# An adaLN block of two Mamba-2 layers and a channel mix: modulated rows made inside the first layer's loop

## What is computed

```python
mod = (silu(c) @ wmod).reshape(8, 6, 1, 512)
sa, ca, ga, sb, cb, gb = (mod[:, n] for n in range(6))
ga = (2 * (ga >= 0) - 1) * maximum(abs(ga), 0.25)      # gb likewise
h = layernorm(x) * (1 + ca) + sa
x = x + ga * mamba_layers(h)           # 2 layers, each: h + mamba2(layernorm(h) * w + b)
h = layernorm(x) * (1 + cb) + sb
x = x + gb * channel_mix(h)            # receptance, key, value products, token shift
```

## Time and profile before

| | us |
|---|---|
| time, median of 3 runs | 4278.69 |
| lowest and highest of them | 4275.23, 4281.79 |
| the profiled execution's own time | 4276.1 |
| its span, first to last instruction | 4274.3 |
| PE busy | 4005.1 (94%) |
| DVE busy | 3465.9 (81%) |
| ACT busy | 2899.9 (68%) |
| POOL busy | 2026.9 (47%) |

### The profile page before, as it was taken

How to read it: one execution, slowest core, us unless ns; L and a number is a source line. 1 busy time by engine, 2 the same in 40 slices (tenths; PEclk the granted TensorE clock), 3 DMA queues, 4 the chain that set the end, 5 groups by cost and what they waited for, 6 DMA issues and landing times. The chain is left out here.

```text
span 4274.3 us, 100194 instructions
## 1 busy us (share of the span) xinstructions
PE 4005.1 (94%) x38872; PEld 3600.5 (84%) x38872; DVE 3465.9 (81%) x5227; ACT 2899.9 (68%) x4898; POOL 2026.9 (47%) x1572
## 2 busy tenths in 40 slices
PE   4599999999999999969999999999999996799999
PEld 1599999899999999958999999999999995577777
DVE  8688888888888888868888888888888885666664
ACT  4577777677777777747777777777777773666664
POOL 7344444444444444424444444444444444566664
PEclk6799999999999999979999999999999998899999
DMA  8400000000000000020000000000100002222220
GB/s 327 142 31 31 31 31 31 31 31 31 31 31 31 31 33 32 26 96 29 31 31 31 31 31 31 31 33 35 37 31 31 31 26 85 82 97 97 85 83 33
DMA packets 115764, 220.03 MB, mean 51 GB/s; under 512 B 10792, under 2 KB 20520, under 8 KB 114472
## 3 DMA queue, kind: packets, MB, share of 16 engines
q1 hardware_dynamic: 115376, 214.25, 14.1%
HBM read 146.97 MB, written 67.24 MB: 50 GB/s over the span
## 5 line engine op out<-in xcount | busy, mean ns | idle before, releaser
L508 PE MATMUL l_ring<-l_u_hi,l_wi_lo 128*128 128x256 f32 x4608 | 1318.2, 286 | 22.2 <-ACT l_raw L754 12.4
L508 PE MATMUL l_ring<-l_u_lo,l_wi_hi 128*128 128x256 f32 x4608 | 1296.6, 281 | 0.0
L508 PE MATMUL l_ring<-l_u_hi,l_wi_hi 128*128 128x256 f32 x4608 | 1296.0, 281 | 0.0
L1008 DVE SCALAR_TENSOR_TENSOR l_xc<-l_raw,l_prm,l_xc 128x256 f32<-128x256 f32 x1536 | 958.3, 668 | 96.4 <-ACT l_xc L763 78.2
L508 PEld LDWEIGHTS l_ring<-l_u_hi,l_wi_lo 128*128 128x128 f32 x4608 | 873.1, 189 | 48.3 <-issue 16.9
L508 PEld LDWEIGHTS l_ring<-l_u_lo,l_wi_hi 128*128 128x128 f32 x4608 | 874.0, 190 | 11.7
L1199 POOL TENSOR_TENSOR l_g<-l_g 128x512 f32<-128x512 f32 (+2 forms) x384 | 355.6, 926 | 1096.1 <-ACT l_g L824 1076.0
L508 PEld LDWEIGHTS l_ring<-l_u_hi,l_wi_hi 128*128 128x128 f32 x4608 | 873.9, 190 | 0.0
L1170 POOL TENSOR_TENSOR l_rhs<-l_cum,l_small 32x1024 fp32r<-32x1024 f32 x256 | 497.5, 1952 | 154.1 <-PE l_wide L570 103.8
L1190 POOL TENSOR_TENSOR l_g<-l_g,l_zs 128x1024 f32<-128x1024 f32 x128 | 306.0, 2391 | 449.9 <-DVE l_g L1055 448.5
L508 PE MATMUL l_ring<-l_wo_hi,l_g_lo 128*128 128x512 f32 x1024 | 414.0, 404 | 18.9 <-DVE l_g_lo L1060 11.3
(11 more groups left out here) (168 smaller groups left out, 8060.3 us busy)
## 6 DMA issues: line engine op xcount, KB each, us to landing
l_hn<-h_scratch SPq DMA_DIRECT2D x64, 512.0 KB, 3.8
l_res<-h_scratch SPq DMA_DIRECT2D x128, 256.0 KB, 3.6
h_scratch<-l_res SPq DMA_DIRECT2D x128, 256.0 KB, 2.1
m_rows<-in_x SPq DMA_DIRECT2D x16, 1024.0 KB, 9.3
h_scratch<-m_rows SPq DMA_DIRECT2D x16, 1024.0 KB, 7.0
f_x<-in_x SPq DMA_DIRECT2D x16, 1024.0 KB, 5.6
f_h<-h_scratch SPq DMA_DIRECT2D x16, 1024.0 KB, 8.0
out<-f_x SPq DMA_DIRECT2D x64, 256.0 KB, 2.0
```

Source lines behind the costliest of these rows:

```text
L508: last = nc.tensor.matmul(out, a, c, start=(k == 0), stop=(k == n - 1))
L1008: ins = nc.vector.scalar_tensor_tensor(out=acc, in0=raw[:, (s + c) % 2, k, tap:tap + TB], scalar=prm_sb[:, w:w + 1], in1=acc, op0=ALU.mult ...
```

## The change

`prologue` is replaced by `modulation`, which makes only the six products and the terms from them, in the order `ga, gb, sb, cb, sa, ca`, and puts scale and shift of the first half at places 0 and 1 of `mod_dram`. While these run, it loads the nine input pieces of layer 0 into four staging buffers of its own and splits them on ACT and DVE into `wi_hi` and `wi_lo`, which now outlive the layers.

Layer 0 reads `x` itself. For each tile it makes the statistics of the raw rows (`raw_stats` on DVE), the inverse deviation and the offset (`raw_inv_std`, `raw_offset` on POOL), the raw normalise (`raw_normalise` on ACT), and multiplies by a scale row and adds a shift row (`modulate` on POOL); the two rows come by a transfer from `mod_dram`, one after the other into one buffer `mod_row`. SP stores the modulated tile to `h0` (`keep`), from where it is read again as the residual. The residual buffer `res` has room for 128 rows, before for 256. In layer 0 the places of `sum_parts`, `row_stats`, `normalise` and `inv_std` differ from before.

The channel mix loads its first tile in two halves; POOL makes the first half of `x + ga*h` and DVE the second, and the splits of the three matrices stand behind the first norm.

```diff
+def modulation(nc, sems, cT, wmod, in_w, wi_hi, wi_lo, cst, mod_dram, cols_dram, nseq):
+    order = (2, 5, 3, 4, 0, 1)
...
+        def _(sp):
+            sp.dma_start(c_sb[:], cT).then_inc(s_c, 16)
+            for k, n in enumerate(order):
+                sp.dma_start(w_sb[:, n], wmod[:, :, n * DM:(n + 1) * DM]).then_inc(s_w[k], 16)
+            sp.dma_start(ident[:], cst[:, K_ID:K_ID + P]).then_inc(s_id, 16)
+            for n, k in enumerate(OPENING):
+                if n >= 4:
+                    sp.wait_ge(s_wlo, n - 3)
+                sp.dma_start(stage[:, n % 4], in_w[:, :, piece(k)]).then_inc(s_stage[n % 4], 16)
+            sp.wait_ge(s_term, 6)
+            sp.dma_start(mod_dram.rearrange("b (s d) -> b s d", s=6), mod_sb[:]).then_inc(s_kept, 16)
+            sp.wait_ge(s_cols, 1)
+            sp.dma_start(cols_dram.rearrange("b p k -> p b k"), cols_sb[:]).then_inc(s_kept, 16)
...
+            for k, term in enumerate((gate, gate, shift, scale, shift, scale)):
+                term(k, order[k])
+                if k >= 2:
+                    weight_low(2 * k - 4)
+                    weight_low(2 * k - 3)
...
@@ mamba_layer, SP
+            def keep(b, s):
+                i = NB * b + s
+                kept = src[bass.ds(i * TB, TB), :]
+                sp.wait_ge(s_add, NPAIR * (i + 1))
...
             def body(b, s, n1, n2):
...
+                sp.wait_ge(s_store[1], 16 * i)
+                sp.dma_start(res[:], src[bass.ds(row, P), :]).then_inc(s_res[0], 16)
+                if first and n2:
+                    nxt2, nxt3 = ahead(b, s, 2), ahead(b, s, 3)
+                    sp.wait_ge(s_mul, NPAIR * (i + 3))
+                    load_row(nxt2[0], 1, mod_row[:])
+                    keep(*nxt2)
+                    if not (isinstance(b, int) and b == nseq - 1 and s == NB - 3):
+                        load_row(nxt3[0], 0, mod_row[:])
+                sp.wait_ge(s_out, NPAIR * i + 1)
+                sp.dma_start(dst[bass.ds(row, P), :], res[:]).then_inc(s_store[0], 16)
+                sp.wait_ge(s_store[0], 16 * (i + 1))
+                sp.dma_start(res[:], src[bass.ds(row + P, P), :]).then_inc(s_res[1], 16)
...
@@ mamba_layer, ACT
                 new_state(b, s, 0, 1)
+                if first and n2:
+                    raw_normalise(*ahead(b, s, 2))
                 decays(b, s, 1, 0)
...
@@ mamba_layer, DVE
             def normalise(b, s):
+                if first:
+                    dve.wait_ge(s_kept, 16 * (NB * b + s + 1))
...
                 matrices(b, s, 0, 0)
+                if first and n2:
+                    raw_stats(*nxt2)
...
                 matrices(b, s, 1, 0)
+                if first and n1:
+                    sum_parts(*nxt)
                 low_g(b, s, 0)
-                if n2:
+                if n2 and not first:
                     row_stats(*nxt2)
...
                 if n2:
-                    normalise(*nxt2)
+                    if first:
+                        row_stats(*nxt2)
+                    else:
+                        normalise(*nxt2)
                 mean_square(b, s, 0)
...
                     taps(*nxt, 2)
+                if first and n2:
+                    normalise(*nxt2)
+                if n1:
                     taps(*nxt, 3)
...
             def norm_all(b, s):
+                if first:
+                    raw_stats(b, s)
                 row_stats(b, s)
                 normalise(b, s)
@@ mamba_layer, POOL
+            def modulate(b, s, scale_row, shift_row, rows):
+                m = NB * b + s
+                scale_loaded, shift_loaded = rows
+                pool.wait_ge(s_row, scale_loaded)
+                for t in range(NPAIR):
+                    pool.wait_ge(s_xnorm, NPAIR * m + t + 1)
+                    nc.gpsimd.tensor_tensor(hn[:, t, :], hn[:, t, :], scale_row, ALU.mult).then_inc(s_mul, 1)
+                pool.wait_ge(s_row, shift_loaded)
+                for t in range(NPAIR):
+                    pool.wait_ge(s_mul, NPAIR * m + t + 1)
+                    nc.gpsimd.tensor_tensor(hn[:, t, :], hn[:, t, :], shift_row, ALU.add).then_inc(s_add, 1)
...
@@ channel_mix
+            for half in range(2):
...
+                sp.dma_start(x[:, 0, t], x_in[rows, :].rearrange("(t p) d -> p t d", p=P)).then_inc(loaded, 16)
+                sp.dma_start(h2[:, 0, t], h_in[rows, :].rearrange("(t p) d -> p t d", p=P)).then_inc(loaded, 16)
...
-            pe.wait_ge(s_wlo, 3)
+            pe.wait_ge(s_wlo, 1)
...
             normalise(0, 0)
+            weight_high(0)
...
             row_stats(0, 0)
             dve.wait_ge(s_cst, 32)
+            dve.wait_ge(s_offset, 1)
+            weight_low(0)
...
             row_stats(0, 1)
+            weight_low(1)
+            weight_low(2)
```

More of the change, by code:

```diff
@@ L122, in prologue @@
-        s_mag, s_sgn, s_post, s_turned, s_cols = sem("mag"), sem("sgn"), sem("post"), sem("turned"), sem("cols")
-        s_kept = sem("mod_kept")
-        s_spread, s_shift = sem("spread"), sem("shift")
-        s_load = [sem(f"load{k}") for k in range(BUF)]
-        s_store = [sem(f"store{k}") for k in range(BUF)]
-        s_bn, s_mv, s_var, s_rstd, s_off, s_offset = (
-            sem("bn"), sem("mv"), sem("var"), sem("rstd"), sem("off"), sem("offset"))
-        s_norm, s_mul, s_add = sem("norm"), sem("mul"), sem("add")
+        ps = ctx.enter_context(nc.psum_tensor("m_ps", [P, 6, DM], F32))
@@ new lines, in _ @@
+            for k, n in enumerate(order):
+                pe.wait_ge(s_w[k], 16)
+                for d in range(KD):
+                    last = nc.tensor.matmul(ps[0:nseq, n, :], sc_sb[:, d, :], w_sb[:, n, d, :],
+                                            start=(d == 0), stop=(d == KD - 1))
+                last.then_inc(s_mod, 1)
+            pe.wait_ge(s_id, 16)
+            pe.wait_ge(s_term, 4)
+            for k in range(2 * KD):
+                d = (k % KD) * P
+                last = nc.tensor.transpose(ps_t[:, k * nseq:(k + 1) * nseq], mod_sb[:, 3 + k // KD, d:d + P],
+                                           ident[0:nseq, 0:nseq])
@@ L210, in _ @@
+            last.then_inc(s_turned, 1)
         @block.scalar
         def _(act):
-            def normalise(b):
-                act.wait_ge(s_offset, b + 1)
-                for t in range(NT):
-                    row = rows[:, b % BUF, t, :]
-                    nc.scalar.activation(row, row, ACT.Identity, bias=offset[:, b % 2, t:t + 1],
-                                         scale=rstd[:, b % 2, t:t + 1]).then_inc(s_norm, 1)
-            def keep_shift(b):
-                act.wait_ge(s_spread, b + 1)
-                act.wait_ge(s_add, max(NT * (b - 1), 0))
-                nc.scalar.copy(shift[:, b % 2, :], ps[:, b % 2, :]).then_inc(s_shift, 1)
@@ L224, in _ @@
             act.wait_ge(s_c, 16)
             nc.scalar.activation(sc_sb[:], c_sb[:], ACT.Silu).then_inc(s_silu, 1)
-            normalise(0)
-            keep_shift(0)
-            for b in range(1, nseq):
-                normalise(b)
-                keep_shift(b)
+            for n, k in enumerate(OPENING):
+                act.wait_ge(s_stage[n % 4], 16 * (n // 4 + 1))
+                nc.scalar.activation(wi_hi[:, :, piece(k)], stage[:, n % 4], ACT.Identity).then_inc(s_whi, 1)
         @block.vector
@@ L479, in _ @@
                                  ).then_inc(s_stage[n % 4], 16)
+            if first:
+                keep(0, 0)
+                load(b0, 1)
+                keep(0, 1)
             def body(b, s, n1, n2):
@@ L882, in _ @@
             conv_in(b0, 0, 2, 2)
+            if first:
+                raw_normalise(0, 1)
             silu_x(b0, 0, 1)
@@ L918, in split_low @@
                 kind, k = pieces[n]
+                if first and kind == "in":
+                    return
                 dve.wait_ge(s_whi, n_all * layer + n + 1)
@@ L1218, in body @@
                     moving(*nxt, 0)
+                if n2 and first:
+                    inv_std(*nxt2)
+                if n1:
                     moving(*nxt, 1)
@@ L1346, in _ @@
             load_ga(0, 0)
-            load(0, 0)
+            for half in range(2):
+                t = slice(half * early, (half + 1) * early)
+                rows = slice(half * early * P, (half + 1) * early * P)
+                loaded = s_load[0] if half else s_half
+                sp.dma_start(x[:, 0, t], x_in[rows, :].rearrange("(t p) d -> p t d", p=P)).then_inc(loaded, 16)
+                sp.dma_start(h2[:, 0, t], h_in[rows, :].rearrange("(t p) d -> p t d", p=P)).then_inc(loaded, 16)
             sp.dma_start(small[:], cst[:, K_ID:NCST]).then_inc(s_cst, 16)
```

357 lines of the change are left out of this document (163 added, 194 removed).

## The result

The changed kernel takes 4355.93 us (median of four runs, 4346.07 to 4361.72), the kernel before 4278.08 beside it: 1.018 times as long, interval 1.0164 to 1.0196. Forecast were 4300 us and a range of 4235 to 4350. The side was right, the size was not: 78 us instead of 21. The profiled execution, at 4361.7 us, is the slowest of the four and 5.8 us above their median; its span is 4359.9 us and its mean clock 0.966. So differences between the two traces add up to 85.6 us, not to 78.

What follows compares the result with a forecast made beforehand. The prediction took PE to bound the loops, with 0.8% idle, and the prologue as time removable whole. Its terms, -90 + 12 + 3 + 105 - 9 = +21 us on 4276.1, gave about 4300 us, range 4235 to 4350.

Steps and rivals of the forecast that it cites:

- The sum: Whole kernel: all forecast gains and costs added, +21 us on 4276.1 of the profiled execution.
- the waits in that loop: Layer 0's loop: second `low_g` 3.6 us late a tile, PE waiting for `finish` and it; +105 us over 30 tiles.
- X: Six DVE taps in a layer 0 tile: their time above 2.71 us beside POOL's operations, put at 3.7 us.
- the channel mix: Channel mix opening: half loads and splits moved behind the norm bring the first product about 9 us sooner, -9 us.
- The openings: Start of kernel and layer 0: `modulation` for the prologue, -90 us; work ahead of layer 0's loop, +12 us.
- The first half of a tile: Layer 0's loop, first half of each tile: added statistics, normalise and multiplies cost 0.1 us a tile, +3 us.
- the full block: Rival, six taps: five POOL operations block at full length, 5.43 us; loop costs 159 us, 4354 us in all; chance 0.12.
- the rival that was given 0.04: Layer 0's loop: idle PE loses its clock, making the likeliest case up to 20 us worse, 4320; chance 0.04.
- the likeliest case: Whole kernel: taps and POOL operations go by turns, 4300 us; chance 0.47.
- the buffer costs nothing: Both layers: single `res` buffer leaves 16 us, enough for a store and a load of 256 KB; no cost.
- The chain: Layer 0 tile, from the six taps to `finish`: `finish` starts at 1075.3 + X, before at 1076.44.
- the normalise between the taps: Layer 0 tile, DVE: `normalise` between taps 2 and 3 adds 1.0 us on the path to the second `low_g`.

Runs made afterwards that it cites:

- e3: Changed kernel with one added wait: in layer 0's loop POOL starts the first `moving` only after DVE's `y_read` behind the six taps; 4305.21 us, ratio 1.0071.
- e8: e6 with nine more filler products on PE ahead of `proj(7)`, so both PE waits are filled; 4327.76 us, ratio 1.0117.
- e6: Changed kernel with seven filler products on PE ahead of the second output product in layer 0's loop, results overwritten; 4346.95 us, ratio 1.0170.
- e1: Changed kernel with the shift row in a place of its own, loaded a tile earlier, so the adds avoid the six taps; 4248.57 us, ratio 0.9945.
- e4: Changed kernel with the whole channel mix of the kernel before; 4351.96 us, ratio 1.0185.
- e2: Changed kernel with POOL's `inv_std` of tile i+2 moved behind `moving` 1 and `inv_rms` in layer 0's loop; 4295.6 us, ratio 1.0045.
- e5: e1 with the old places of `row_stats`, `sum_parts`, `normalise` and `inv_std` in layer 0's loop; 4212.84 us, ratio 0.9860.
- e7: e5 with output products in both layers doing the eight products with `g_lo` last; 4195.47 us, ratio 0.9818.

## Why the prediction was wrong

The sum said +21 us; the two traces differ by +85.6. Of the 65 us between, the clock in layer 0's loop is 31, a cost that the sum put at nothing; the waits in that loop are 23 (131 for 108), since X was 1.5 us a tile too small, which is 45, while the tile's other terms came out smaller than forecast; the channel mix is 10. The openings and layer 1 make up the small rest.

**The openings**: right. -93.5 for -90; the first product 9.7 us later for 9.7; +13.4 in all for +12.

**The first half of a tile**: right that it costs nothing; forecast was 0.1 us a tile more, measured 0.36 less. The first `low_g` starts 21.81 us behind the first instruction of DVE's tile (1124.24 - 1102.43), before 22.17 (1062.73 - 1040.56). POOL waits 3.20 us for the shift row, and the adds start at 1125.10, with the taps, as forecast.

**X, the excess of the six taps**: the term of the sum that failed first and most. It was put at 3.7 us, "5.43 - 5 x 0.33", for five POOL operations by turns. The turns are right; the list was not complete. The text says of `moving(nxt, 0)` that it "is done before that, so it is free". It is done before `inv_std`, but it is done beside the sixth tap, because the adds pushed the squares and it by their own length. A sixth operation of 1.9 us less 0.33 gives 5.3; measured 5.18, and e3, which takes that one operation away, measures 1.63 for it. That X lies near the full block's 5.43, and the time near that rival's 4354 us, is chance: the rival had five operations at full length and no lower clock. With X = 5.2 the forecast's own chain puts the second `low_g` 5.1 us late; measured are 4.36 (47.65 us behind the first instruction of DVE's tile, before 43.29). Of the 0.7 between, 0.36 is the first half, and 0.3 that `gate` starts ahead of `finish` and holds the taps 2 up less: from `finish` to `low_g` pass 8.11 us, before 7.41, where 1.0 more was forecast.

e3 is the kernel with the X that was forecast: 6.26 - 2.71 = 3.55. It takes 4305 us, where 4300 were forecast, and its 31 tiles 104 us more than before, forecast 108. So the one operation that was missing from the list is worth 51 of the 56 us by which the time was missed: 1.5 us a tile, 45 in all, and the falls of the clock in 16 of 28 tiles. That the numbers meet so well is in part luck: e3's short tiles are 2.7 us longer, not 3.5 (30 x 2.7 = 81), and the other 23 us lie in its longer tiles, mostly those with the lower clock, which the sum did not have.

By the Trainium skill ("SBUF — State Buffer", SBUF: two separate sides) a DVE instruction with two SBUF inputs and a GpSimd instruction exclude each other for the whole instruction. The trace agrees in kind: the taps wait and the adds are stretched too (1.47 us for 1.26), while operations with a PSUM input keep their length. It doesn't let one add up full lengths: the six POOL operations take 7.3 us alone (2 x 1.26, 2.91 and 1.89), and the taps lost 5.18, so some 0.36 us of each overlapped (0.38 in e3, 0.44 for the three squares before).

**The clock**: the rival that was given 0.04 and up to 20 us came true beside the likeliest case, not instead of it, and costs 31 us (e8). This is nearly half of the error, and the step that failed was to treat it as an alternative. Waits of 3.5 us a tile were forecast in a loop that had none; the fall followed them, as e6 and e8 show, and its price belonged in the sum.

**The sum**, put right: -93.5 + 13.4 + 131 + 31 + 4 = 86, of the spans. The 4 are the channel mix (1.4) and the last tile of layer 1 (2.6). That tile takes 50.16 us at a mean clock of 0.74, before 47.54 at 0.83; in e1 the last tile of layer 1 takes 47.26 us with the same single `res` buffer, so the buffer costs nothing, as forecast.

**The channel mix**: -9 was wrong, 0 is right (e4). Two steps failed. The 6.8 us from the statistics to the norm of tile 0 were read as the work of the splits; with the splits away they are 6.6, by an idle time of POOL whose cause stays open, so the norm comes 4.4 us sooner and not 9.5. And only the first tile was followed: the splits that left its path were put in the path of the second.

**The chain** over `row_stats`, `inv_std`, `moving(nxt, 1)` and `inv_rms` was right in every step (e2 came out at the number expected), and the normalise between the taps takes the 1.0 us that was forecast (0.99 in the trace). What each of the moved operations is worth alone is not shown: e5 puts all of them back at once, for 1.3 us a tile.

## What to carry to other kernels

When an operation is put on an engine's queue beside work that it must take turns with, list everything that it pushes, not only itself: what was beside harmless work may now be beside the sensitive one. A loop that ran at full clock while its engine never waited paid twice for a new wait here, once for the wait and once for the clock. And most of the gain of the moved prologue was there to be had: with the shift row in a place of its own, the adds beside readers of PSUM, and the order kept, the same change gives 1.4% (e5), with the low part last 1.8% (e7).
